# The mask's complement on ScalarE, and the residual of three image pairs in four GpSimd steps instead of six

## The reference, cut to what matters

```python
out1 = conv2d(x, conv2_w, conv2_b, PAD)
mask = jax.nn.sigmoid(conv2d(x, mask_w, mask_b, PAD))
xm = x * mask
q = conv2d(xm, q_w, q_b, 0)
# k and v from the padded xm; softmax over a 3x3 window
out2 = out2 + attn[..., idx][:, None] * v[:, :, i:i + H, j:j + W]
return out1 * mask + (1.0 - mask) * out2
# and outside:
return residual + out
```

## Time and profile before

| | us |
|---|---|
| median of 3 runs (lowest, highest) | 209.73 (209.48, 210.34) |
| the profiled execution | 211.26 |
| its span, first to last instruction | 209.5 |
| busy: TensorE, VectorE, ScalarE, GpSimd | 184.3, 161.2, 119.3, 70.5 |
| GpSimd's complement, 4 instructions | 7.1 |
| GpSimd's first residual step, 4 instructions | 5.1 |

### The profile page before, as it was taken

One profiled execution on the slowest core, in us unless ns is written; L12 is line 12 of the kernel. 1 busy time (PEld: TensorE's weight loads), 2 busy tenths in 40 slices (PEclk: granted clock), 3 DMA queues, 4 the chain that ended last, 5 costly groups with the idle time before them and its releaser, 6 DMA issues.

```text
span 209.5 us, 5365 instructions
## 1 busy us (share of the span) xinstructions
PE 184.3 (88%) x2155; PEld 103.0 (49%) x2163; DVE 161.2 (77%) x382; ACT 119.3 (57%) x251; POOL 70.5 (34%) x62
## 2 busy tenths in 40 slices
PE   1699879979998999899999978999899998899972
PEld 1349339323354555734657345743323345565831
DVE  6798799988768879598498985993838576992682
ACT  2176273655249742956785463678545583966850
POOL 7500803250220402750008611850044003670390
PEclk9999999988999999999999999999999999999999
DMA  5422031001501000001000040001001000000002
GB/s 191 90 56 59 2 99 51 3 0 33 150 19 46 7 5 10 3 3 39 3 0 0 3 150 10 9 0 50 0 3 50 3 0 10 5 8 8 5 2 103
DMA packets 10154, 6.75 MB, mean 32 GB/s; under 512 B 7248, under 2 KB 8496, under 8 KB 10128
## 3 DMA queue, kind: packets, MB, share of 16 engines
q1 hardware_dynamic: 9888, 5.82, 10.4%
q10 hardware_dynamic: 240, 0.58, 0.7%
HBM read 3.30 MB, written 1.05 MB: 21 GB/s over the span
## 4 chain that ended last, share of the span: by engine, by line
PE 46%; DVE 25%; ACT 14%; issue 7%; DMA 3%; POOL 1%; SPq 1%; DVEq 0%; ACTq 0%
PE ps L1452 18%; PE ps L1365 5%; DVE sh_in L316 4%; ACT sh_x L608 4%; PE ps L1489 4%; PE ps L1372 4%; PE ps L1399 3%; ACT xw L703 3%; PE ps L1524 3%; DMA w3b<-in_w_gi 3%; DVE sh_ln L316 2%; PE ps L1535 2%; PE ps L1513 2%; DVE ln_out L965 2%; POOL ln_s L473 1%
## 5 line engine op out<-in xcount | busy, mean ns | idle before, releaser
L1452 PE MATMUL ps<-sh_ln,w_gi 96*64 96x512 f32 x192 | 45.1, 615 | 2.8 <-DVE sh_ln L316 1.7
L473 POOL TENSOR_TENSOR ln_s<-ln_s,neg_half 128x16 f32<-128x16 f32 x7 | 20.4, 2908 | 55.6 <-DVE ln_s L944 55.6
L608 ACT ACTIVATE sh_ln<-ln_out 32x512 f32<-32x512 f32 (+2 forms) x46 | 25.6, 557 | 12.2 <-DVE ln_out L965 5.3
L1452 PEld LDWEIGHTS ps<-sh_ln,w_gi 96*64 96x64 f32 x192 | 14.6, 140 | 27.6 <-issue 27.5
L1399 PEld LDWEIGHTS ps<-w_qk,sh_ln 128*128 128x128 f32 x192 | 22.2, 192 | 3.6 <-issue 2.5
L1399 PE MATMUL ps<-w_qk,sh_ln 128*128 128x128 f32 x192 | 23.3, 278 | 0.4 <-issue 0.4
L1489 PE MATMUL ps<-sh_in,w_in 96*32 96x256 f32 x384 | 22.6, 381 | 0.7 <-DVE sh_in L316 0.7
L1365 PE MATMUL ps<-busy 128*128 128x512 bf16 x65 | 18.5, 419 | 1.7 <-issue 1.0
L608 ACT ACTIVATE sh_x<-x 32x496 f32<-32x496 f32 (+1 forms) x20 | 12.3, 616 | 12.3 <-DVE x L1090 12.1
L1489 PEld LDWEIGHTS ps<-sh_in,w_in 96*32 96x32 f32 x384 | 11.7, 110 | 11.3 <-DVE sh_in L316 2.9
L498 POOL TENSOR_TENSOR omm<-ones,msk 128x512 f32<-128x512 f32 x4 | 7.1, 1780 | 21.6 <-DVE msk L1166 21.6
(11 more groups left out here) (142 smaller groups left out, 339.1 us busy)
## 6 DMA issues: line engine op xcount, KB each, us to landing
sh_ln<-ln_out SPq DMA_DIRECT2D x27, 64.0 KB, 2.1
x_res<-in_x SPq DMA_DIRECT2D x4, 256.0 KB, 2.8
out_x<-out_s SPq DMA_DIRECT2D x4, 256.0 KB, 2.0
x_norm<-in_x SPq DMA_DIRECT2D x3, 256.0 KB, 2.9
kc<-in_shape_consts ACTq DMA_DIRECT2D x1, 450.0 KB, 4.7
w3b<-in_w_gi SPq DMA_DIRECT2D x1, 288.0 KB, 5.2
x_norm<-in_x SPq DMA_DIRECT2D x2, 128.0 KB, 2.9
xm<-xm SPq DMA_DIRECT2D x8, 25.5 KB, 1.9
```

Source lines behind the costliest of these rows:

```text
L473: nc.gpsimd.tensor_tensor(ln_s[n][:, 3, :], ln_s[n][:, 2, :], neg_half[:, :], ALU.pow)\
L608: return nc.scalar.activation(o, i, ACT.Copy)
L1452: mm = nc.tensor.matmul(ps[EC * h:EC * h + EC, GI_BANKS[n], :], w_gi[:, dy, n % 2, :], xs[:, n // 2, y:y + H // 2, 0:W], start=(dy == 0), ...
```

## The change

ScalarE computes the complement from `th` in one instruction, as -0.5 th + 0.5, so it no longer hangs on `msk`. It stands in front of `pv_evac` for pairs 0 and 1, behind `out1_evac` for pair 2, and in front of `key_windows` for pair 3. For pairs 0 to 2 the residual is rewritten as (x2 + out1) + (1 - mask)(out2 - out1): `residual` keeps one step, and `final` has three instead of two. Pair 3 keeps its three steps of `residual` (now `masked_residual`), because VectorE's `final` for it is unchanged. `out1` gets two buffers, since it is now read until `final`. The waits follow.

The core of the diff (lines cut that only rename or count):

```diff
-        out1 = sb("out1", [P, 2 * BLK])
+        out1 = [sb(f"out1_{n}", [P, 2 * BLK]) for n in (1, 2)]
...
+        g_om = signal("mask_complement_done", 1)
+        g_res = signal("residual_steps", [1] * (PAIRS - 1) + [3], start=1)
+        g_fin = signal("final_steps", [3] * (PAIRS - 1) + [2], start=1)
...
-            def complement(pair):
-
-                g = g_res
-                pool.wait_ge(g_xm.sem, g_xm.at(pair, 1))
-                if pair > 1:
-                    pool.wait_ge(g_fin.sem, g_fin.done(pair - 2))
-                nc.gpsimd.tensor_tensor(omm[pair % 2][:, :], ones[:, :], msk[:, :], ALU.subtract).then_inc(g.sem, 1)
-
             def residual(pair):
...
-                nc.gpsimd.tensor_tensor(res[pair % 2][:, :], out1[:, :], flat(x2[pair % 2][:, :, :]), ALU.add).then_inc(g.sem, 1)
-                pool.wait_ge(g.sem, g.at(pair, 1))
-                nc.gpsimd.tensor_tensor(dif[:, :], omm[pair % 2][:, :], out1[:, :], ALU.mult).then_inc(g.sem, 1)
-                pool.wait_ge(g.sem, g.at(pair, 3))
+                if pair > 1:
+                    pool.wait_ge(g_fin.sem, g_fin.done(pair - 2))
+                nc.gpsimd.tensor_tensor(res[pair % 2][:, :], out1[pair % 2][:, :], flat(x2[pair % 2][:, :, :]), ALU.add)\
+                  .then_inc(g.sem, 1)
+
+            def masked_residual(pair):
+
+                g = g_res
+                residual(pair)
+                pool.wait_ge(g_om.sem, g_om.done(pair))
+                nc.gpsimd.tensor_tensor(dif[:, :], omm[pair % 2][:, :], out1[pair % 2][:, :], ALU.mult).then_inc(g.sem, 1)
+                pool.wait_ge(g.sem, g.at(pair, 2))
                 nc.gpsimd.tensor_tensor(res[pair % 2][:, :], res[pair % 2][:, :], dif[:, :], ALU.subtract)\
...
-                nc.gpsimd.tensor_tensor(dif[:, :], pv[:, :], omm[pair % 2][:, :], ALU.mult).then_inc(g.sem, 1)
+                nc.gpsimd.tensor_tensor(dif[:, :], pv[:, :], out1[pair % 2][:, :], ALU.subtract).then_inc(g.sem, 1)
                 pool.wait_ge(g.sem, g.at(pair, 1))
+                pool.wait_ge(g_om.sem, g_om.done(pair))
+                nc.gpsimd.tensor_tensor(dif[:, :], dif[:, :], omm[pair % 2][:, :], ALU.mult).then_inc(g.sem, 1)
+                pool.wait_ge(g.sem, g.at(pair, 2))
...
-                if not is_first(pair):
-                    act.wait_ge(g_res.sem, g_res.at(pair - 1, 1))
                 nc.scalar.activation(th[:, :], ps[:, mask_bank(early), :], ACT.Tanh, bias=half_bm[:, 0:1], scale=0.5)\
...
-                act.wait_ge(g_res.sem, g_res.before(pair))
-                nc.scalar.activation(out1[:, :], ps[:, conv2_bank(early), :], ACT.Identity,
+                if pair > 1:
+                    act.wait_ge(g_fin.sem, g_fin.done(pair - 2))
+                nc.scalar.activation(out1[pair % 2][:, :], ps[:, conv2_bank(early), :], ACT.Identity,
...
+            def complement(pair):
+
+                if pair > 1:
+                    act.wait_ge(g_fin.sem, g_fin.done(pair - 2))
+                act.wait_ge(g_th.sem, g_th.done(pair))
+                nc.scalar.activation(omm[pair % 2][:, :], th[:, :], ACT.Copy, bias=0.5, scale=-0.5).then_inc(g_om.sem, 1)
...
                 x2_planes(pair + 1)
+                complement(pair)
                 pv_evac(pair)
...
             out1_evac(but_last)
+            complement(but_last)
...
             k_evac(last, True)
+            complement(last)
             key_windows(last)
```

More of the change, by code:

```diff
@@ L268, in build @@
         g_o1 = signal("out1_in_sbuf", 1)
-        g_res = signal("residual_steps", 4, start=1)
-        g_fin = signal("final_steps", 2, start=1)
+        g_om = signal("mask_complement_done", 1)
+        g_res = signal("residual_steps", [1] * (PAIRS - 1) + [3], start=1)
+        g_fin = signal("final_steps", [3] * (PAIRS - 1) + [2], start=1)
         g_out = signal("out_stored", 16, start=1)
@@ L529, in step @@
             def step(pair, norm):
-                complement(pair)
                 residual(pair)
@@ L576, in _ @@
             but_last, last = PAIRS - 2, PAIRS - 1
-            complement(but_last)
             inorm_rstd(last)
@@ L581, in _ @@
             residual(but_last)
-            complement(last)
-            residual(last)
+            masked_residual(last)
             final(but_last, last)
```

## The result

The changed kernel takes 211.94 us in the median of 6 runs (211.18 to 212.90), the kernel before, on the same chip, 210.06 (6 runs, 209.48 to 210.72). The ratio is 1.0091, with a 95% interval of 1.0057 to 1.0125: slower by 1.2 to 2.6 us. The forecast was 2.38 us more, 212.1 us. The profiled execution took 211.98 (span 210.1); before it was 211.26 (span 209.5). Ratios here leave out executions more than 1.5% above the fastest of their kernel (two of six in best2, among them the profiled one), medians and ranges count all.

What follows compares the result with a forecast made beforehand. The chain of waits was mostly TensorE (46%) and VectorE (25%), GpSimd 1%. Terms 0.54 + 0.60 + 0.45 - 0.20 + 0.54 + 0.45 = 2.38 us on the median 209.73 gave 212.1 us, range 210.7 to 213.2.

Steps and rivals of the forecast that it cites:

- What bounds the kernel: Chain of waits: TensorE 46%, VectorE 25%, ScalarE 14%, GpSimd 1%; fewer GpSimd instructions worth next to nothing by themselves.
- The freed port wins: Rival, chance 0.08: VectorE loses some 3.4 us of holds by GpSimd's complements and residual steps, giving 208.9 us.
- Complement, pairs 0 and 3: +0.54 each: ScalarE's complement delays pv through VectorE's sum in pair 0, and the key windows in pair 3; +0.54 us each.
- Third step, pair 0: +0.60: Pair 0's third final step holds VectorE's copies, 0.98 later; less 0.38 slack, mask, xm and halo +0.60 us.
- Third step, pair 1: +0.45: Pair 1's third final step holds VectorE's L1107, delaying TensorE's matmul L1481 by 0.45 us; low end 0.05.
- `act_in`: -0.20: Before pair 3's mask, act_in no longer held by GpSimd; the tanh is late next, so the gain is 0.20 us.
- The end: +0.45: GpSimd's added final step of pair 2 makes VectorE's last operation wait for it instead of TensorE; +0.45 us.
- Nothing held: Rival, chance 0.22: added third steps hold nothing; only ScalarE, the tanh's 0.20 and the end count: 1.33, 211.1 us.
- The general rival: GpSimd and VectorE meet at other places throughout, and no single edit gives the loss back; no chance given.

Runs made afterwards that it cites:

- best2: comp_only with GpSimd's masked residual steps of pairs 1 and 2 and pair 0's final and store moved later; ratio 0.9844 to the kernel before, 208.46 us.
- hidden: Changed kernel with ScalarE's complements moved to where it waits anyway (pairs 0 and 1 behind the head's exponential, pair 3 before key copies); ratio 1.0041 to the kernel before.
- p0_old: hidden with pair 0 alone back to three-step residual and two-step final; from pair 1's x2 sum to the end 106.88 us, 0.52 less than hidden.
- own_dif: Changed kernel with a separate buffer and signal for VectorE's last two operations; from pair 1's x2 sum to the end 108.25 us, 0.46 less.
- comp_only: Kernel before with only the complement moved to ScalarE, where it waits, plus a GpSimd wait in pair 3's residual; ratio 0.9957 to the kernel before.
- flip: own_dif plus a wait before GpSimd's second residual step of pair 3; from pair 1's x2 sum to the end 108.28 us, the same as own_dif.

## Why the prediction was right, step by step

- *What bounds the kernel.* Right: ten GpSimd steps taken from the middle, with three added in `final`, gave back only 0.27 (0.20 at `act_in`, 0.07 behind L936, where I had counted 0). "The freed port wins" fell: of those holds the chain passed only `act_in`, and there the tanh became the wait.
- *Complement, pairs 0 and 3: +0.54 each.* Measured +0.53 and +0.52; hidden took both away. One takes 0.63 alone and the next operation starts 0.52 to 0.54 after it began, so the spacing of the exponentials was the row to use, not one operation's length.
- *Third step, pair 0: +0.60.* The copies came 0.98 later, as worked out: they end 20.08 us after the sum before and 21.59 after, 1.51 apart, of which 0.53 is the complement. The mask used up 0.47 where I had allowed its idle 0.38: it now follows the operation ahead of it without a pause (L1039 ends at 124.16, the mask starts at 124.08); +0.51. p0_old showed the cause.
- *Third step, pair 1: +0.45.* The hold was as predicted: L1117's end, 158.01, is 158.43 in the frame of before, where I had put 158.44. The term was too high for what follows: I let L1114 start after L1107's end, but L1124 (the same operation after) started at 157.92, 0.09 ahead of that end. TensorE's matmul, in the frame of before, came at 158.92, not 159.13, which takes off 0.21; it was at 158.61 before and not at the chain's 158.68, which adds 0.07. Measured +0.31.
- *`act_in`: -0.20.* Measured -0.20; the tanh became the wait.
- *The end: +0.45.* Measured +0.37, and 0.46 less in own_dif, where the wait is gone.

The sum was 2.38 and is 1.98; the time, +1.9 (1.2 to 2.6), can't tell the two apart. "Nothing held" would have been 1.33, with no hold on copies of 0.42 or on L1117; the traces show both holds. The general rival falls too: hidden, p0_old and own_dif give back 1.31, 0.52 and 0.46, each close to its terms; they were not run together. What I did not price lay outside the sum: holds that the kernel before already had, above all at pair 0 and in the softmax product, were worth 2.1 us (best2), more than the whole change.

The Trainium skill ("SBUF — State Buffer", "Who interferes with whom") says that the order of issue decides who blocks and that the first holds the shared ports for its whole instruction. The traces agree for the softmax product of 480 numbers (0.66 when it is first, 1.65 when it is second) and for L1117 (1.17 under GpSimd's step, 0.17 alone). They don't for GpSimd's power, which also reads SBUF: under its 2.90 L1107 took 0.17.

## What to carry to other kernels

Before an engine is relieved, look at when its steps come, not at how many there are: the ten steps removed from the middle gave back 0.27 in all, and the three added at the end of a pair cost 0.51, 0.31 and 0.37, because each met another engine's chain. Work moved to an idle engine is free only where that engine waits, so place it just ahead of a wait (hidden: 1.31 us). And follow a waiting instruction back through everything queued ahead of it on its own engine: the mask waited for the tanh, the tanh's engine for copies, and those for an operation that GpSimd held.

## What was not expected of the hardware

- A start 0.2 us earlier or later reverses which of two operations is held, and moves 1 us: GpSimd's step starts 0.14 ahead of the softmax product in after, which takes 1.65, and 0.06 behind it in comp_only and flip, where it takes 0.66.
- The prologue reached the `x2` sum of pair 1 between 100.35 (own_dif) and 103.99 (best2), 3.64 us apart. It begins with a wait for the load of `vec`: in the chain 4.22 us in own_dif, 6.13 in best2, 1.91 more. And the same 24 matmuls took 1.70 more in best2, so the two make up 3.61 of it. From the chain of best2:

```profile
44.70 7.07 PE ps L1474 x24
```

From that of own_dif:

```profile
42.75 5.37 PE ps L1464 x24
```

TensorE's granted clock was 0.50 of full speed (its lower level, 1.2 GHz) in best2 from 46 to 48, and 1.00 in own_dif from 42 to 50. In both, TensorE had sat idle for 1.73 just ahead of these matmuls; why the clock fell in one only, these traces don't say. Effects below 1 us are better read from a mark inside the trace than from single times.
